# A residual block of two 3x3 convolutions: GpSimd forms the low parts of x's outer planes for rows 15 to 27

## What is computed

```python
out = relu(bn(conv3x3(x, w1), g1, b1, m1, v1))
out = bn(conv3x3(out, w2), g2, b2, m2, v2)
return relu(out + x)
```

## Time and profile before

| what | value |
|---|---|
| median of 3 runs | 589.64 us (589.43 to 589.86) |
| the profiled execution | 589.92 us, of which the span is 588.2 us |
| TensorE, matmuls | busy 569.0 us (97%) |
| VectorE | busy 551.6 us (94%) |
| ScalarE | busy 494.3 us (84%) |
| GpSimd | busy 46.3 us (8%) |
| mean granted TensorE clock | 0.989 of full speed |

### The profile page before, as it was taken

One profiled execution on the slowest core, in us unless ns is written; L12 is line 12 of the kernel. 1 busy time (PEld: TensorE's weight loads), 2 busy tenths in 40 slices (PEclk: granted clock), 3 DMA queues, 4 the chain that ended last, 5 costly groups with the idle time before them and its releaser, 6 DMA issues.

```text
span 588.2 us, 9134 instructions
## 1 busy us (share of the span) xinstructions
PE 569.0 (97%) x3090; PEld 551.9 (94%) x3090; DVE 551.6 (94%) x476; ACT 494.3 (84%) x763; POOL 46.3 (8%) x52
## 2 busy tenths in 40 slices
PE   6769999999999999999999999999999999999997
PEld 3669999999999999999999999999999999999996
DVE  5789999999999999999999999999999999999984
ACT  4678898888889888889888888988888988888885
POOL 6700000000000000000000000000000000000000
PEclk9789999999999999999999999999999999999999
DMA  8345554454554435555444555444554544441012
GB/s 286 103 113 143 142 161 147 102 151 141 150 158 144 140 107 148 159 141 161 146 105 146 141 155 154 146 132 116 150 156 141 168 144 112 137 142 55 28 56 109
DMA packets 31680, 79.90 MB, mean 136 GB/s; under 512 B 2609, under 2 KB 19121, under 8 KB 31665
## 3 DMA queue, kind: packets, MB, share of 16 engines
q1 hardware_dynamic: 26912, 66.11, 31.0%
q0 software_dynamic: 4608, 13.31, 14.7%
q10 hardware_dynamic: 144, 0.29, 0.2%
HBM read 54.01 MB, written 25.69 MB: 135 GB/s over the span
## 4 chain that ended last, share of the span: by engine, by line
PE 92%; ACT 1%; DVE 1%; DMA 1%; issue 1%; POOL 1%; ACTq 0%
PE psum L676 92%; DMA x_inner<-x_dram 1%; POOL w_mat L217 0%; DVE x_lo L404 0%; DVE t_outer L442 0%; ACT h_hi L557 0%; ACT x_hi L537 0%; ACT z L567 0%; DVE ti_lo L450 0%; POOL out_sb L190 0%; ACT z L566 0%; ACT out_sb L595 0%; ACT psum L547 0%; ACT ti_hi L557 0%; DVE psum L418 0%
## 5 line engine op out<-in xcount | busy, mean ns | idle before, releaser
L676 PE MATMUL psum<-x_hi,w_hi 128*128 128x392 f32 (+2 forms) x512 | 178.5, 349 | 9.9 <-DVE x_lo L404 9.9
L676 PE MATMUL psum<-x_hi,w_lo 128*128 128x392 f32 (+2 forms) x512 | 175.4, 343 | 0.0
L676 PE MATMUL psum<-x_lo,w_hi 128*128 128x392 f32 (+2 forms) x512 | 175.1, 342 | 0.0
L418 DVE TENSOR_TENSOR psum<-psum,z 128x784 f32<-128x784 f32 (+1 forms) x128 | 127.2, 994 | 18.2 <-PE psum L676 11.1
L676 PEld LDWEIGHTS psum<-x_hi,w_hi 128*128 128x128 f32 x512 | 97.2, 190 | 16.5 <-issue 10.4
L676 PEld LDWEIGHTS psum<-x_lo,w_hi 128*128 128x128 f32 x512 | 97.2, 190 | 0.5
L676 PEld LDWEIGHTS psum<-x_hi,w_lo 128*128 128x128 f32 x512 | 97.1, 190 | 0.5
L595 ACT ACTIVATE out_sb<-psum 128x784 f32<-128x784 f32 x64 | 52.9, 827 | 48.6 <-PE psum L676 48.6
L676 PE MATMUL psum<-ti_hi,w_hi 128*128 128x392 f32 x256 | 89.6, 350 | 1.9 <-ACT psum L547 1.9
L676 PE MATMUL psum<-h_lo,w_hi 128*128 128x392 f32 x256 | 87.3, 341 | 0.0
L676 PE MATMUL psum<-h_hi,w_hi 128*128 128x392 f32 x256 | 87.2, 341 | 0.0
(11 more groups left out here) (66 smaller groups left out, 812.4 us busy)
## 6 DMA issues: line engine op xcount, KB each, us to landing
x_sb<-x_dram SPq DMA_DIRECT2D x32, 814.0 KB, 5.0
out_dram<-out_sb SPq DMA_DIRECT2D x64, 392.0 KB, 2.8
x_inner<-x_dram SPq DMA_DIRECT2D x32, 406.0 KB, 3.3
x_inner<-x_dram POOLq DMA_DIRECT2D x32, 406.0 KB, 5.1
z<-w_dram ACTq DMA_DIRECT2D x1, 288.0 KB, 3.9
out_sb<-w_dram SPq DMA_DIRECT2D x1, 288.0 KB, 6.3
bn<-params_dram SPq DMA_DIRECT2D x1, 132.0 KB, 3.7
```

The lines of the kernel that those rows point to most:

```text
L418: nc.vector.tensor_tensor(psum[:, half, EVEN:ODD + 1, 0:width], t1, z[:, half, :, 0:width], ALU.add).then_inc(joined[conv], 1)
L676: ins = nc.tensor.matmul(psum[:, half, bank, first:first + (j1 - j0) * WQ], w[:, i, far, :], moving, start=not onto and at == 0, stop=at = ...
```

## The change

GpSimd gets a new function, `split_beside`, called twice per image. Each call subtracts for one of the two outer planes (`place` 0 or 1) the rows 15 to 27: 13 rows of 28, 364 elements a partition. DVE's `split_x("outer")` keeps the rows 0 to 14 of both planes. Image n's DVE part is still formed in step n-1; the GpSimd pieces follow in step n. The first piece waits for the end of `sum_hidden(s-1)`, behind which DVE has `join(2, s-2, 1)`; the second piece waits for the same semaphores as `join(1, s, 0)` and for the end of the DVE instruction ahead of it. A new semaphore `beside` counts the pieces. DVE's `outer_x(n)`, which overwrites `x_outer`, waits for both pieces of image n-1, and TensorE waits for both before `outer_products(1, s, ..., 1)`.

```diff
+        beside = sem("beside")
...
+            def split_beside(n, k, place):
+
+                rows = slice(HALF1[1][0], NQ)
+                full = x_full("outer", k)[0][:, place, rows]
+                pool.wait_ge(xhi_ready["outer"], n + 1)
+                pool.tensor_tensor(x_lo[:, k % 2, place, rows], full, x_hi[:, k % 2, place, rows].bitcast(F32),
+                                   ALU.subtract).then_inc(beside, 1)
+
             def step(s, k):
                 if is_step(s, 0):
                     low_weights(pool, "all2")
+                if there_is(s, s):
+
+                    if there_is(s, s - 1):
+                        pool.wait_ge(th_ready["t1"], s)
+                        pool.wait_ge(xlo_ready["outer"], s + 1)
+                    split_beside(s, k, 0)
+                    if there_is(s, s - 1):
+                        pool.wait_ge(hlo_ready["t1"], s)
+                        pool.wait_ge(z_ready[1], 2 * s + 1)
+                        pool.wait_ge(inner[1], 4 * s + 2)
+                        wait(pool, out_ready, 2 * (s - 2) + 1)
+                    split_beside(s, k, 1)
                 if there_is(s, s + 2):
 
                     add_odd(s + 2, (k + 2) % 4)
...
             def outer_x(n, k):
 
                 wait(dve, xlo_ready["outer"], n)
+                wait(dve, beside, 2 * n)
...
                 dve.wait_ge(xhi_ready[which], n + 1)
-                nc.vector.tensor_tensor(x_part(x_lo, k, places), full,
-                                        x_part(x_hi, k, places).bitcast(F32),
+                rows = slice(0, HALF1[1][0]) if which == "outer" else slice(0, NQ)
+                nc.vector.tensor_tensor(x_part(x_lo, k, places)[:, :, rows], full[:, :, rows],
+                                        x_part(x_hi, k, places)[:, :, rows].bitcast(F32),
                                         ALU.subtract).then_inc(xlo_ready[which], 1)
...
                         pe.wait_ge(xlo_ready["outer"], s + 1)
+                        if half == 1:
+                            pe.wait_ge(beside, 2 * s + 2)
                         outer_products(1, s, k % 2, half)
```

## The result

The changed kernel takes 590.84 us (median of 7 runs, 589.30 to 591.99), the kernel before beside it 589.43 us (7 runs, 588.87 to 589.86): a ratio of 1.0021, 95% interval 1.0011 to 1.0031. That is 1.2 us more by the ratio and 1.4 us by the medians, at the bound of what can be told from no change. The forecast was 589.9, the range 588.9 to 593.6.

What follows compares the result with a forecast made beforehand. The prediction took a circle of waits through TensorE and DVE, 17.39 us a period, as the bound. Periods 0 plus start 0.3 on 589.92 gave 590.2, less 0.28 to the median: 589.9 us, range 588.9 to 593.6.

Steps and rivals of the forecast that it cites:

- The circle of waits and its critical part: TensorE's first groups, relu_out, then DVE from join(1, s, 0) through join(2, s-1, 0): 17.39 us; only DVE time there lengthens periods.
- The outer split is in the slack, gain 0: DVE's outer split stands behind the critical part, ahead of 0.48 us idle; sparing 0.8 us a period gains nothing.
- The price of a piece: One GpSimd subtraction of 364 elements takes 0.96 us, bounds 0.83 to 1.06.
- the room of 1.09 us: GpSimd's piece 1 may end up to 1.09 us after join(1, s, 0) starts without delaying DVE; cost 0.
- Rival 2: GpSimd's piece asks over 0.95 us after the join's start and blocks outer_hidden: 26 us more, 616 us; chance 0.05.
- hand-over of some 0.14: A blocked DVE instruction ends some 0.14 us sooner after GpSimd's end than its own length, so that overlap is free.
- The start, +0.3 us: First steps: image 1's first piece holds DVE's split 0.8 us, net cost 0.3, bounds -0.5 and +0.9.
- rival 1: GpSimd's piece ends later than 1.09 us after the join's start, stalling the split behind: up to 3.6 us, 593.5; chance 0.30.

Runs made afterwards that it cites:

- the two fills: Kernel before plus one 256-element VectorE fill in each of 30 steps: behind the outer split 589.17 us, ratio 1.0006; behind the inner split 596.79 us, ratio 1.0128.
- the inner planes: Changed kernel, but GpSimd forms rows 15 to 27 of the inner planes, not the outer, from image 2 on: 584.57 us, ratio 0.9917 to the kernel before.

## Why the prediction was right, and where it was off

- *The circle of waits and its critical part*: shown by the two fills (0 against 0.26 us a step) and by the inner planes (4.5 us less by the medians beside each other, 4.9 by the ratio, for the same rows taken off DVE). A busy share of 94% said nothing about it.
- *The outer split is in the slack, gain 0*: shown; 0.69 and 0.38 us of idle time stand where the work was. I had put the first at 0.8, without what the late relu leaves to sum_hidden.
- *The price of a piece*, 0.96 us: measured 0.90 to 0.91, nearer to this than to 0.83. For 560 elements it is 1.30, so 0.16 us and 2.04 us per thousand elements.
- *No contention beside a join; the room of 1.09 us*: shown at both sides, by pieces of 0.90 (no cost) and of 1.30 (0.24 us, the whole overhang).
- *Rival 2, the piece that misses the join*: did not happen, and its mechanism is real; I had priced it at 0.87 a period and it is 0.71: a piece of 0.90, of which the hand-over of some 0.14 that I had used elsewhere had to be taken off here too (0.76; the last 0.05 is open).
- *The start, +0.3 us*: this term was mis-sized, and for the wrong piece. Measured are +1.2 to +1.4 for the start. I charged the first piece of image 1 ("of the 0.8 us that the piece holds the split, I take 0.3 as net"); with that piece alone the kernel is at 1.0002. The loss needs image 0's pieces. I took GpSimd's low weights as done at 28.66, as in the one execution that I had read. They are done when TensorE's first groups, at half speed, and ACT let them be: the pieces ended at 29.6, 30.4 and 30.8 us in three traces, and image 1, which I had at 34.1, started at 33.31, 34.09 and 34.52. In the executions with the clock at 0.994 the time is 589.3 to 589.6 us, 0.3 to 0.6 under my sum; in the others it goes up to 592. So the step that failed is "I take 0.3 as net", whose bounds of -0.5 and +0.9 held neither this path nor the clock.
- *The range*: the time fell inside it by luck. The forecast's own range was 589.1 to 590.8, and its upper end was added up wrongly: 589.64 + 0.9 is 590.5. The measured 590.84 lies above both, and inside 588.9 to 593.6 only because that was widened for rival 1, the overhang, which did not happen.

How the loss is shared between the clock's late rise in the first groups, its falls behind the waits in steps 0 and 1, and the pieces' own delay is read from three traces of different executions and was not tested by an experiment that moves only one of them. What decides when the clock rises in a given execution stays open.

## What to carry to other kernels

Before work is moved off an engine that is busy for 94%, follow one period's circle: find the instruction of the bound engine that comes late, go back from releaser to releaser until the circle closes, and see whether the work to be moved is in it. In this kernel, a VectorE instruction with an operand in PSUM was a place beside which GpSimd could work on SBUF at no cost, if the piece started with it and was no longer than it; what overhung cost its full length, and a piece that came behind the next instruction cost most of its own (0.71 of 0.90 us). Leave the first steps as they are when pieces are handed to another engine, or follow the new chain there from its beginning: what stood off the chain (here the low weights, behind TensorE's first groups at half speed) can come to stand on it.

## What the runs showed of the hardware

- The granted clock fell behind waits of TensorE of 3.51 and 2.74 us in one execution (591.45 us) and behind 3.51 us in another (590.17), where it stayed up behind 2.62; it stayed up behind 3.15 and 2.61 us in a third (589.55). Executions of the changed kernel fall into groups some 1 us apart that go with their mean granted clock.
- The half speed at the beginning lasts differently long in the same kernel: TensorE's first 18 matmuls took 4.86 us in one execution and 5.69 in another. Whether that reaches the end is a matter of the chain: 0.80 us of it did in the changed kernel.
- A GpSimd instruction that waits for VectorE's memory access shows this as a longer record, not as idle time: 1.58 us in place of 0.90. So does VectorE's (2.55 in place of 1.84).
- A wait of TensorE of up to some 0.15 us leaves no idle time in the records of the matmuls. It shows as one wide and one narrow distance of weight loads (0.38 and 0.11 us in the earlier trace rows), and 31 of them were worth 4.4 us.
